# Two sorted expert stages of a four-layer transformer kernel loop over 71 blocks instead of 72

## What is computed

```
# layer 2
router_logits = jnp.einsum('bth,eh->bte', x, router_w)
topk_values, topk_indices = jax.lax.top_k(router_logits, TOP_K)
topk_weights = jax.nn.softmax(topk_values, axis=-1)
h1 = jax.nn.gelu(jnp.einsum('bth,efh->btef', x, w1) + b1, approximate=False)   # f = 512
expert_outputs = jnp.einsum('btef,ehf->bteh', h1, w2) + b2
mixed_output = sum over the two chosen experts of topk_weights * expert_outputs
# layer 3
moe_out = jnp.einsum('te,teh,ehd->td', cw, jax.nn.silu(g) * u, w2)   # h = 256; g, u from w1, w3
return moe_out + shared_out                                         # a ninth expert, for every token
```

## Time and profile before

| what | value |
|---|---|
| time, median of 3 runs | 1712.88 us |
| lowest and highest of them | 1707.56 and 1715.41 us |
| profiled execution, first to last instruction (span) | 1643.5 us |
| mean granted TensorE clock | 0.927 of 2.4 GHz |
| PE / DVE / ACT / POOL busy | 81% / 62% / 57% / 36% |
| first stage's block loop, first gather to last scatter | 1043.9 to 1240.6 us |
| second stage's block loop, first transpose to last scatter | 1502.4 to 1618.7 us |

### The profile page before, as it was taken

How to read it: one execution, slowest core, us unless ns; L and a number is a source line. 1 busy time by engine, 2 the same in 40 slices (tenths; PEclk the granted TensorE clock), 3 DMA queues, 4 the chain that set the end, 5 groups by cost and what they waited for, 6 DMA issues and landing times. The chain is left out here.

```text
span 1643.5 us, 43000 instructions
## 1 busy us (share of the span) xinstructions
PE 1333.4 (81%) x16797; PEld 1113.8 (68%) x16821; DVE 1026.8 (62%) x2574; ACT 942.8 (57%) x2144; POOL 586.4 (36%) x588
## 2 busy tenths in 40 slices
PE   4699999986899998899258975777782888888994
PEld 4588777864688888687225653676671567677994
DVE  5677777774543333789788996633335678853445
ACT  3466555642354444798635642655555889834884
POOL 2233333321000000343147860477772004444662
PEclk9799999998999999999569997899996999978997
DMA  9200000009997000231000001011113001002335
GB/s 317 59 19 19 19 19 19 2 3 135 156 181 70 1 1 1 86 118 58 0 17 18 18 5 52 28 49 49 48 50 126 15 15 41 29 31 56 93 92 175
DMA packets 143529, 94.11 MB, mean 57 GB/s; under 512 B 55776, under 2 KB 130273, under 8 KB 142817
## 3 DMA queue, kind: packets, MB, share of 16 engines
q1 hardware_dynamic: 134368, 72.86, 20.5%
q0 software_dynamic: 8960, 18.50, 3.5%
HBM read 51.20 MB, written 40.12 MB: 56 GB/s over the span
## 5 line engine op out<-in xcount | busy, mean ns | idle before, releaser
L400 POOL TENSOR_TENSOR wide_probs<-wide_probs,wide_key_mask 128x512 f32<-128x512 f32 x64 | 82.8, 1314 | 188.1 <-ACT wide_probs L521 188.1
L1536 POOL DMA_INDIRECT moe_x_rows<-moe_rows,moe_source x72 | 79.6, 1106 | 76.0 <-DVE moe_source L1632 54.4
L739 POOL MEMSET attn_v_bd<- 128x576 f32 x2 | 1.2, 617 | 268.8 <-POOLq L163 268.8
L2228 DVE TENSOR_TENSOR moe_hidden<-banks,moe_gate 128x256 f32<-128x256 f32 x104 | 43.6, 423 | 84.2 <-ACT moe_gate L2427 83.0
L769 POOL TENSOR_TENSOR attn_col_bd<-attn_col_t,group_mask_sb 128x1024 f32<-128x1024 f32 x32 | 60.7, 1897 | 97.0 <-ACT attn_row_t L966 97.0
L3045 ACT ACTIVATE moe_router<-banks,moe_rb_sb 128x512 f32<-128x512 f32 x64 | 41.4, 688 | 91.8 <-PE banks L3149 67.8
L2062 POOL DMA_INDIRECT moe_results<-moe_y_rows,moe_x_rows x72 | 68.9, 958 | 51.8 <-issue 30.1
L1890 POOL DMA_INDIRECT moe_rows<-moe_xhat,moe_slot x64 | 61.9, 967 | 69.1 <-DVE moe_slot L2190 50.1
L843 DVE TENSOR_REDUCE attn_top<-banks 128x32 f32<-128x2048 f32 x32 | 73.1, 2283 | 18.6 <-PE banks L1027 18.6
L995 ACT ACTIVATE attn_probs<-attn_probs 128x1024 f32<-128x1024 f32 x64 | 65.9, 1053 | 27.9 <-DVE attn_probs L872 26.4
L1542 POOL DMA_INDIRECT moe_results<-moe_y_rows,moe_dest x72 | 73.0, 1014 | 22.4 <-issue 20.7
(11 more groups left out here) (434 smaller groups left out, 4313.4 us busy)
## 6 DMA issues: line engine op xcount, KB each, us to landing
moe_rows<-route_empty_sb SPq DMA_DIRECT2D x8, 2624.0 KB, 22.6
attn_ctx<-in_ctx_t SPq DMA_DIRECT2D x48, 128.0 KB, 2.1
moe_x_rows<-moe_rows SPq DMA_DIRECT2D x72, 66.0 KB, 1.9
moe_pack_sb<-in_moe_pack SPq DMA_DIRECT2D x8, 578.0 KB, 3.9
moe_w_sb<-in_moe_w SPq DMA_DIRECT2D x2, 2048.0 KB, 10.1
moe_hot<-moe_results SPq DMA_DIRECT2D x16, 256.0 KB, 6.0
moe_until_back<-moe_results SPq DMA_DIRECT2D x16, 256.0 KB, 5.7
moe_pack_sb<-in_moe_pack SPq DMA_DIRECT2D x9, 384.0 KB, 4.2
```

Of the source, the lines that this page charges most:

```text
L400: nc.gpsimd.tensor_tensor(probs[b.parity][:, :, h2], probs[b.parity][:, :, h2], keys, ALU.mult).then_inc(masked, 1)
L1536: nc.gpsimd.indirect_dma_start(x_rows[s % GATHERS][:], None, rows, bass.IndirectOffsetOnAxis(ap=source[:, s:s + 1], axis=0)).then_inc(gath ...
```

## The change

A constant `FILLED` = (2 * 4096 + 8 * 127) // 128 = 9208 // 128 = 71 is added, and the block loops of all engines in both stages run to `FILLED`. Tables, buffers and DRAM tensors keep the size `BLOCKS`. SyncE's waits on the eight `scattered` semaphores ask each for as many scatters as it now gets: nine for seven of them and eight for the last. The branches marked `gated` in `sparse_experts` are not used by this program.

```diff
--- before.py
+++ after.py
@@ -1399,6 +1399,7 @@
 
 
 BLOCKS = 2 * TILES + EXPERTS
+FILLED = (2 * TOKENS + EXPERTS * (P - 1)) // P
 SLOT_ROWS = BLOCKS * P
 PAD_TOKEN = -SLOT_ROWS % TOKENS
 GATHERS = 8
@@ -1492,10 +1493,10 @@
         CHOSEN, COUNTED, PLACED = 14, 16, 28
 
         order = []
-        for b in range(BLOCKS):
+        for b in range(FILLED):
             order.append((True, b))
-            if gated and TILES * (b + 1) // BLOCKS > TILES * b // BLOCKS:
-                order.append((False, TILES * b // BLOCKS))
+            if gated and TILES * (b + 1) // FILLED > TILES * b // FILLED:
+                order.append((False, TILES * b // FILLED))
         place = {b: n for n, (routed, b) in enumerate(order) if routed}
         items = lambda n: order[n] if 0 <= n < len(order) else None
 
@@ -1512,7 +1513,7 @@
                     sp.wait_ge(xhat_ready, u + 1)
                     sp.dma_start(by_token(rows)[:, u * UNIT:(u + 1) * UNIT], xhat[u % 4][:]).then_inc(rows_stored[u % 4], DMA_INC)
                 for n in range(GATHERS):
-                    sp.wait_ge(scattered[n], BLOCKS // GATHERS * DMA_INC)
+                    sp.wait_ge(scattered[n], len(range(n, FILLED, GATHERS)) * DMA_INC)
                 for u in range(UNITS):
                     part = slice(u * UNIT, (u + 1) * UNIT)
                     for k in range(2):
@@ -1529,8 +1530,8 @@
                 for n in range(4):
                     pool.wait_ge(rows_stored[n], UNITS // 4 * DMA_INC)
                 pool.wait_ge(listed, 1)
-                for s in range(BLOCKS + 9):
-                    if s < BLOCKS:
+                for s in range(FILLED + 9):
+                    if s < FILLED:
                         if s >= GATHERS:
                             pool.wait_ge(turned, s - GATHERS + 1)
                         nc.gpsimd.indirect_dma_start(
@@ -1988,7 +1989,7 @@
         count_bank, spell_bank = core.bank[4], core.bank[5]
 
         order = [(False, t) for t in range(SHARED_FIRST)]
-        order += [(True, b) for b in range(BLOCKS)]
+        order += [(True, b) for b in range(FILLED)]
         order += [(False, t) for t in range(SHARED_FIRST, TILES)]
         place_at = {b: n for n, (routed, b) in enumerate(order) if routed}
         item = lambda n: order[n] if 0 <= n < len(order) else None
```

## The result

The changed kernel takes 1707.76 us (median of 22 runs) against 1715.39 us of the kernel before (22 runs beside them). One of the 22 runs of the changed kernel was slow as a whole, at 4164.9 us, and the ratio leaves it out. The ratio is 0.9955, 95% interval 0.9939 to 0.9971: 7.7 us less, with 5.0 to 10.5 us inside the interval. The forecast was 4.2 us less, 1708.7 us, within 0.5%. That the time fits to 1 us is partly luck. The kernel before came out 2.5 us longer than in the runs that the forecast starts from (1715.39 against 1712.88 us), and the gain 3.5 us larger.

What follows compares the result with a forecast made beforehand. It took GpSimd's gathers and scatters to bound the first stage and TensorE the second; 2.74 + 1.45 = 4.2 us off 1712.88 us gave 1708.7 us, range 1702.5 to 1715 us.

Steps and rivals of the forecast that it cites:

- What bounds each stage: Block loops: GpSimd's gathers and scatters set the first stage's pace, TensorE the second's, with ScalarE close behind.
- Second stage, 1.45 us: Second block loop: one block less saves one TensorE step, 1.45 us, and the tail shifts with it.
- First stage, 2.74 us: First block loop: one gather and one scatter less on GpSimd let the next stage begin 2.74 us earlier.
- the drain: First stage, last gather to last scatter: nine scatters follow, and the length stays 13.20 us.
- My bounds for the sum: Both stages' savings together: between 3.8 and 4.2 us.
- The part outside the span: Median of the runs less the profiled span: 69.4 us, left alone as no row showed it depending on a block.
- My own sign of being wrong: Time outside the profiled span: the forecast would be wrong if it changed by more than 1 us.
- The clock: TensorE's clock in attention: low for longer gives 1717 us, chance 0.07; low for less gives 1702.8 us, chance 0.08.
- The waits: SyncE's wait for eight scatters instead of nine on the last semaphore: cost zero.
- taken back behind the barrier: Rival after the first stage: its gain is lost, only the second's 1.45 us shows, 1711.4 us; chance 0.04.
- covered by the shared tiles: Rival at the kernel's end: TensorE's shared tiles end last, so the change does nothing, 1712.9 us; chance 0.03.
- theory 2: Follow-up expectation, not in the prediction: a surplus over the removed steps, some 3 us, comes from moved code.

Runs made afterwards that it cites:

- e9: Kernel before, 72 blocks, but first-stage TensorE makes one hidden and one output matmul for blocks 68 to 71 instead of four and four; ratio 0.9984.
- e2: Kernel before with only the first stage cut to 71 blocks, the second kept at 72; ratio 0.9975, gain 4.1 us.
- e5: The changed kernel again, no further edit, against the kernel before on a chip with short executions; ratio 0.9958, gain 6.9 us.
- e1: Kernel before again, unchanged, for its profile beside its own time; ratio 0.9996, own time 1642.63 us.
- e6: Kernel before, unchanged, a single execution of the short kind taken for its trace; no ratio given.
- e12: Kernel before, unchanged, compared with itself on the chip where it takes 1717.79 us; ratio 1.0014.
- e11: The changed kernel a third time, no further edit, against the kernel before where that takes 1717.79 us; ratio 0.9948, gain 8.9 us.
- e10: Kernel before, 72 blocks, but second-stage TensorE makes one hidden and one output matmul for blocks 68 to 71 instead of four and two; ratio 0.9973.
- e7: Kernel before with the first stage cut to 68 blocks, the second kept at 72; ratio 0.9915, gain 14.0 us.
- e4: Kernel before with both stages cut to 68 blocks; ratio 0.9903, gain 16.0 us.

## Why the prediction was right, and where its size was off

*What bounds each stage: right.* In the first stage TensorE waits 40.7 us in all for gathered rows, and GpSimd, behind its first gather, for hardly anything (the row of the transposes under e9, and the earlier trace rows); e9 could not test this. In the second, TensorE's step of 1.449 us stood in all eight traces of the short kind beyond the first, to the hundredth, whatever the number of blocks.

*Second stage, 1.45 us: right.* 15.50 to 14.05 us from block 67's transpose to the end of the scatters, and the rest moved with it: the last scatter is 9.70 us behind the last transpose before and after.

*First stage, 2.74 us: too small by 0.1 us, perhaps by up to 0.9 us.* The step was sized well (2.73 to 2.81 us in five traces with 72 blocks). The term that I held fixed was the drain, at 13.20 us. It is not fixed from one execution to the next: it ran from 12.96 to 13.69 us with 72 blocks, was 12.81 and 12.86 us with 71, and 12.98 and 13.36 us with 68. So it doesn't shrink with the count, and the low values of the two traces with 71 blocks may be chance. Step and drain together are 3.6 us for this block in the traces of e2 and e5, and 2.9 us per block over four. With 1.45 us that makes 4.3 us of the gain, or 5.0 us if the first figure is taken. My bounds for the sum, 3.8 to 4.2 us, were too narrow: they came from two neighbouring steps, and the step's spread over the stage is wider (2.57 to 3.15 us in the last six steps of e1 alone).

*"The part outside the span", 69.4 us: wrong.* It is 2 us. It was the difference between two kinds of execution, and it did no harm only because I had left it alone. My own sign of being wrong, a change of that part by more than 1 us, came true. On the chips of the longer kind a block costs 3.05 + 1.81 = 4.9 us and not 4.2 us, and the forecast was against a time of that kind. A span so far from its kernel's median should have been read as a warning that the steps are not those of the timed runs.

*The clock: no sign of the rival where executions are short, open where they are long.* The granted clock between 1265 and 1500 us was 0.92 in e5 as in e6 and in the first trace. The stretches at the lower level do move, but in the kernel before as well: from 1285 to 1290 us it was granted 0.54 in the first trace, 0.85 in e1 and 0.66 in e6. By the rule cited in the prediction (the Trainium skill, TensorE: Matmul & The Clock Gate, section What's actually happening), stretches shift from execution to execution of the same code, and the traces agree.

In the long executions it is another matter. TensorE from 1265 to 1500 us in e6, e12, e11 and e10 (length, busy, granted clock, DMA share, GB/s):

```profile
1265.00:1500.00 235.00, 193.28 (x2677) 0.92 0.09 29
...
1265.00:1500.00 235.00, 183.52 (x2411) 0.81 0.10 33
...
1265.00:1500.00 235.00, 176.87 (x2442) 0.86 0.11 36
...
1265.00:1500.00 235.00, 175.71 (x2436) 0.86 0.11 36
```

The changed kernel had 0.86 (e11) and the kernel before 0.81 (e12), and the stretch between the two loops took 285.4 and 293.1 us. This difference of 7.7 us is most of the 8.4 us between the two spans. The change needn't be its cause, since e10 has 72 blocks and 286.5 us. Over whole runs it is the same: the mean granted clock was 0.909 in e11's 12 runs and 0.905 in the 35 runs of the kernel before beside them, and among those 35 a clock higher by 0.01 goes with a time some 8 us shorter. At that rate, an estimate from these runs, 3.3 of e11's 8.9 us go with the clock. They don't show which of the two causes the other.

*The waits, and the other rivals.* Nothing was taken back behind the barrier: e7's four blocks came through at 14.0 us. And the last block was not covered by the shared tiles: with 68 blocks the last scatter moved up by all of 5.8 us.

*What stays open.* Three comparisons of the change gave 7.7, 6.9 and 8.9 us, and the traces account for 4.3 to 5.0 us. From the first gather to the end of the span, e5 has 1596.4 us and the kernel before 1599.6, 1602.0 and 1599.0 us (first trace, e1, e6), 2.6 to 5.6 us more: the steps again, and not 7.7 us. A surplus of some 3 us is either real or chance. For chance: each of the three intervals contains 5.0 us; e4 has no surplus at all (16.0 us against 16.8); e10 shows a gain of 4.6 us with next to nothing in its edited stretch, and its runs too have a higher granted clock (0.908); and the first gather, which no edit can reach, lies anywhere from 1038.0 to 1045.1 us in fourteen traces. Against it: all three lie on the same side, and taken together, as if they were independent, they give 7.7 us with 5.7 to 9.8 us inside the interval (my estimate from the three), which leaves 5.0 us out. If it is real, it is not a step of either loop, since both were measured by themselves. Two causes stay possible: a clock that the change has moved, and code that runs differently where it now lies (theory 2 in the expectations). Neither was isolated: no kernel here moved the code without removing work.

## What to carry to other kernels

Where a loop's engine is found by its waits, one turn less is worth one step of that engine, and the step can be taken from the trace to a few hundredths of a us; but size the drain behind the loop from several traces, and don't treat it as fixed. Put a profile's span beside its own time and beside the median of the runs before subtracting anything from it: 69 us apart meant here that steps of the timed runs were 12 and 25% longer than those I had read. For a change worth a quarter of a per cent the traces say where it went long before the times say how much. And before an experiment takes work away from one engine, check in a trace that this work comes ahead of the event that is to move: in e9 it came behind it.

## What the runs showed of the hardware

The same kernel took 1643 us on one chip and 1720 us on another (e1, e12: medians of 12 runs), with the parts ahead of the first sorted stage as fast on both. Between e6 and e12, 21.4 us are added from the first gather to the last scatter of the first stage, 30.9 us from there to the first transpose of the second stage, at a granted clock of 0.81 instead of 0.92 (1265 to 1500 us), and 24.5 us from there to the last scatter. In the second stage three steps of four are as fast as before: the median is 1.45 us on either. What is added there are long steps, of 1.9 to 4.9 us, 17 in the 68 of e12 and none in e6's. They come in a rhythm of about four blocks, on TensorE, ScalarE and VectorE close together. In the episode shown under e12, ScalarE stands idle for 2.71 us with a releaser that the profile can't name, VectorE then waits for it (3.43 us), and TensorE for VectorE (0.99 us); TensorE itself waits 0.45 us for nothing that is shown. A step that is long because an engine doesn't get its next instruction would look like this. The Trainium skill (Advanced Engine Details and Errata, section ISA Cache) says that an engine's instruction cache has only two lines of 256 instructions, and a larger size on TensorE. Three things bear on this, and all speak rather against it. The kernel is written out in full everywhere, also in the first 1040 us, which are as fast on both chips. The transfers of instructions are no more in the long execution; queue, packets, MB and share are the same in e6 and in e12:

```profile
q8 instruction: 136, 2.23, 0.6%
```

And the long steps don't keep to fixed places in the code: the first long ones start at blocks 10, 14, 18 and 22 in the first trace of the changed kernel, and at 10, 15, 19 and 23 in e11. No run here varied the code's length or place by itself, so the cause stays open.
